# Interleaving the last feed-forward of a four-stage network with the end of its attention stack

## The chip, the cores and the metric

The kernel runs on one core of one Trainium2 chip. The metric is the device time of one execution in microseconds (us). Before the change its median over three runs is 3018.09 us (3016.32 to 3019.29). The engines are named as the profile names them: PE is TensorE (PEld its weight loads), DVE is VectorE, ACT is ScalarE, POOL is GpSimd, SP is SyncE, which here only issues DMAs.

## The reference, cut to what matters

Four stages follow each other, each added to its input: a Mamba block, a mixture of experts, a stack of six attention layers, and a gated feed-forward whose inputs and weights are quantized to FP4 in blocks of 16. The change concerns the end of the third stage and the whole fourth.

```
# six layers over (4 sequences of the batch seen as) 2 x 1024 tokens, 128 wide, 16 heads of 8
def layer(h, p):
    w_avg = softmax(q k^T / sqrt(8)).mean(heads)
    new_w = softmax(w_avg + rel)
    h1 = ln(h + new_w @ h);  h2 = ln(h1)
    ff = relu(h2 @ w1.T + b1) @ w2.T + b2
    return ln(h2 + ff)
x = x + stack(layernorm(x))
# last stage; fp4(x): per block of 16, scale = max|x| / 6, round x / scale to E2M1, times scale
xn = layernorm(x)
h  = silu(fp4(xn) @ fp4(w_gate).T) * (fp4(xn) @ fp4(w_up).T)     # 352 wide
x  = x + fp4(h) @ fp4(w_down).T
```

## The kernel before, in words

There are 2 sequences of 1024 tokens, that is 16 tiles of 128 tokens (X holds them). Every engine has its own program, written out in order; semaphores tie them together.

**The attention stack.** One loop over `STEPS` (line 172) steps runs on each engine. A step q of the first 768 (`PAIRS`) handles a pair of head groups of a block of query rows: PE computes the scores (line 650) into three PSUM tiles in turn, DVE takes the negated row maximum (1251), ACT the exponentials with their sum (922), DVE the reciprocal of the sums (1261), POOL a small diagonal matrix from it (1498), and PE the weighted sum over heads (661). All that follows per block, per tile and per half batch ("half", 4 tiles) is cut into pieces. Three tables, `BLOCK_DUE`, `TILE_DUE` and `HALF_DUE` (lines 150 to 171), say at which step after its block, tile or half is through, and at which of two places within a step, each engine issues each piece; `due()` (175) reads them. An engine executes its pieces strictly in that order. The pieces of a half, in the order of their dependencies:

- `evac` (ACT 884), `rel0 rel1` (POOL 1440), `turn` (DVE 1204), `attend0` to `attend3` (PE 594), `add1 bn0` (DVE 1209 to 1216): the second softmax and its product, per tile.
- `pv0 pw0 ln00..ln07` (POOL 1418 to 1456): statistics and application of the first layer norm; `bn10..13` (DVE 1228), `pv1 pw1 ln10..ln17` (POOL): the second; `hb0 hb1` (POOL 1460): adds the bias of the feed-forward.
- `h2t` (PE 599), `h2c` (ACT 887), `ff1_00` to `ff1_31` (PE 606, four quarters), `re0` to `re3` (ACT 895, one after each quarter; a quarter waits for the `re` before it, since all use PSUM bank 7), `ff2_0` to `ff2_7` (PE 613), `add2` (DVE 1220), `bn20..23` (DVE 1228), `pv2 pw2 ln20..ln27` (POOL): the layer's own feed-forward and third layer norm.
- in the last layer `fin` (POOL 1482) adds the result to X; it stands where `sp00` of the other layers stands, 42 steps after the half is through.

There are 24 halves (`HALF_N`); the last four (20 to 23) are the last layer's. Half 23 is the last half batch: it is through with step 767, so all its pieces come after the last pair, each waiting for the one before. SP loads the last stage's weights (1579, 1580) once the scores of half 22 are all made.

**After the loop** the engines do, in order: DVE quantizes the gate and up weights (768 columns) and the down weights (352 columns) with `fp4_dve` (1230 to 1242: nine instructions, 1234 the block maximum, 1235 to 1237 the scale, 1238 the division, 1239 to 1242 the rounding by adding and subtracting a power of two); POOL multiplies each by its scale (`requant_pool`, 1487); PE transposes them (686, 689), ACT copies them out (932 to 935). Then comes fence 3: every engine signals PE, PE signals back (522), and SP waits too. The fence is there because the last stage's buffers (XN, XQ, XQT, QA, QP, HH, HQ ...) lie in memory that the attention's tiles also use.

**The last stage** runs in whole phases. Layer norm of all 16 tiles (`ln_dve`, `ln_pool`, `ln_act`: statistics on DVE 987 to 998, the power -1/2 on POOL 1322, half the tiles applied on ACT 753); four quantizations of 4 tiles each (DVE `quant`, POOL 1487); four transposes (PE 699, ACT 941); then 8 groups of 2 tiles: `gate_up` (PE 709, ACT Silu 949, DVE product 1288), quantization of the 704 columns (DVE, then POOL 1487) and `down` (transposes PE 721, copies ACT 958 and 959, matmuls PE 728, residual add on DVE 1294). A store of 2 tiles per group (SP 1613) ends it.

```
            for grp in range(NG + 1):
                if grp + 1 < NG:
                    gate_up(grp + 1)
                if grp < NG:
                    e.wait_ge(s["swiglu"], 2 * grp + 2)
                    quant(4 + grp, ...)
                if grp:
                    down(grp - 1)
```

Of the kernel before, what the change touches and what calls it, by code (L numbers as in the profile page):

```python
# [20 lines left out]

LNQ = {"ln5": 0}
# [204 lines left out]
class Chain:  # L227
# [1474 lines left out]
```

## Time and profile before

| what | value |
|---|---|
| median of three runs | 3018.09 us |
| the profiled execution | 3021.18 us |
| its span, first to last instruction | 3019.3 us |
| mean granted clock of PE | 0.963 of full |
| busy: PE, DVE, ACT, POOL | 2612.8, 2557.9, 2365.6, 1331.9 us |
| last exponential of the attention ends | 2832.8 us into the span |
| from there to the end | 186.5 us |

The profiled execution took 3.1 us more than the median; 1.9 us of it lie outside the span. "Granted clock" is the share of its full rate at which PE ran in a stretch: 1.00 is 2.4 GHz and 0.50 is 1.2 GHz, the two levels there are, and a value between is a mix. Two engines can be busy at once, so shares of a stretch don't add up to its length.

### The profile page before, as it was taken

What the parts mean: (1) busy time and instruction counts of PE and PEld (TensorE: products, weight loads), DVE (VectorE), ACT (ScalarE), POOL (GpSimd) and SP (SyncE); (2) the same over time, 40 slices, a digit from 0 to 9 for tenths busy, and PEclk for the clock granted to TensorE, in tenths of its full rate; (3) what the DMA queues carried; (4) which work ended last, traced back from release to release, by engine and by line L of the source; (5) the groups of instructions that cost most, each with busy time, mean ns of one, the idle gap of its engine ahead of it and who ended that gap; (6) DMA issues with size and microseconds to landing.
All of it is one profiled execution on the core that took longest, in us unless ns stands there. A gap on an engine that the chain in (4) does not pass through costs nothing.

```text
span 3019.3 us, 80481 instructions
## 1 busy us (share of the span) xinstructions
PE 2612.8 (87%) x31023; PEld 1417.2 (47%) x31023; DVE 2557.9 (85%) x4100; ACT 2365.6 (78%) x4152; POOL 1331.9 (44%) x3035
## 2 busy tenths in 40 slices
PE   6888899978989889998899988898988998888636
PEld 3444576734444444444444444444444444444324
DVE  4888736489999999989998989989999998999556
ACT  5877543469889989988998989889998998999511
POOL 2111202124445664455654556645566545655421
PEclk8999999989999999999999999999999999999857
DMA  2000001322322213212223223222232232210000
GB/s 61 1 1 1 15 1 22 47 63 26 44 38 34 44 33 43 44 31 41 44 33 44 36 36 49 37 34 40 32 59 33 29 44 33 39 18 10 1 0 14
DMA packets 86783, 94.55 MB, mean 31 GB/s; under 512 B 4592, under 2 KB 84736, under 8 KB 85632
## 3 DMA queue, kind: packets, MB, share of 16 engines
q1 hardware_dynamic: 86400, 89.41, 19.0%
q8 instruction: 245, 4.01, 0.6%
q14 instruction: 138, 1.13, 0.2%
HBM read 69.47 MB, written 19.92 MB: 30 GB/s over the span
## 4 chain that ended last, share of the span: by engine, by line
PE 46%; issue 17%; DVE 15%; POOL 6%; ACT 6%; DVEq 0%; POOLq 0%; ACTq 0%
PE bank L661 12%; PE bank L650 10%; DVE NM L1251 9%; PE bank L594 5%; ACT E L922 4%; PE bank L576 3%; PE bank L566 3%; PE bank L606 3%; PE bank L613 2%; PE bank L631 1%; DVE st L1228 1%; POOL acc L1440 1%; POOL HB L1456 1%; POOL HB L1453 1%; ACT acc L884 1%
## 5 line engine op out<-in xcount | busy, mean ns | idle before, releaser
L1251 DVE TENSOR_REDUCE NM<-bank 128x1 f32<-128x1024 f32 x1536 | 1809.0, 1210 | 128.2 <-PE bank L650 123.3
L922 ACT ACTIVATE E<-bank,NM 128x1024 f32<-128x1024 f32 x1536 | 1709.8, 1116 | 223.2 <-DVE NM L1251 222.0
L661 PE MATMUL bank<-E,dg 128*32 128x256 f32 x12288 | 970.8, 385 | 96.8 <-ACT acc L884 73.7
L650 PE MATMUL bank<-KS,QS 128*32 128x512 bf16 x12288 | 961.6, 383 | 79.4 <-ACT E L922 50.6
L1498 POOL TENSOR_TENSOR dg<-mask,RZ 128x64 f32<-128x64 f32 x768 | 225.0, 293 | 833.7 <-DVE RZ L1261 713.0
L661 PEld LDWEIGHTS bank<-E,dg 128*32 128x32 f32 x12288 | 346.0, 109 | 428.6 <-issue 192.5
L650 PEld LDWEIGHTS bank<-KS,QS 128*32 128x32 bf16 x12288 | 320.2, 96 | 481.5 <-ACT E L922 296.6
L1440 POOL TENSOR_TENSOR acc<-acc,rel 128x256 f32<-128x256 f32 x384 | 273.1, 732 | 150.9 <-ACT acc L884 150.7
L922 ACT ACTIVATION_READ_ACCUMULATOR E<-bank,NM 128x1 f32 x1536 | 304.7, 198 | 0.0
L594 PE MATMUL bank<-H,ET 128*128 128x129 f32 x1536 | 225.3, 289 | 7.8 <-issue 4.8
L594 PEld LDWEIGHTS bank<-H,ET 128*128 128x128 f32 x1536 | 188.1, 192 | 89.7 <-issue 80.7
L1192 DVE SCALAR_TENSOR_TENSOR EO<-bank,OH,EO 128x128 f32<-128x128 f32 x256 | 72.0, 344 | 132.2 <-PE bank L576 132.0
L870 ACT ACTIVATE HS<-bank,cst 128x512 f32<-128x512 f32 x128 | 87.3, 686 | 112.4 <-PE bank L566 112.3
L1204 DVE STREAM_TRANSPOSE ET<-acc 128x512 f32<-128x512 f32 x192 | 133.4, 695 | 20.7 <-POOL acc L1440 20.7
L503 PE MATMUL bank<-hC,ident 128*128 128x512 f32 x256 | 142.7, 641 | 8.4 <-DVE XS L1042 7.1
L576 PEld LDWEIGHTS bank<-W,HS 128*128 128x128 f32 x1024 | 124.2, 192 | 30.4 <-issue 29.7
L825 ACT ACTIVATE dBT<-UT,BT 128x256 f32<-128x256 f32 x256 | 108.6, 495 | 25.7 <-PE bank L487 25.2
L884 ACT ACTIVATE acc<-bank 128x512 f32<-128x512 f32 x192 | 114.6, 597 | 15.0 <-PE bank L661 5.8
L576 PE MATMUL bank<-W,HS 128*128 128x128 f32 x1024 | 124.6, 275 | 0.0
L566 PE MATMUL bank<-RTr,W 128*128 128x512 f32 x256 | 121.5, 597 | 0.1
L613 PEld LDWEIGHTS bank<-WL,UB 128*128 128x128 f32 x768 | 96.9, 195 | 51.8 <-issue 49.6
L613 PE MATMUL bank<-WL,UB 128*128 128x128 f32 x768 | 119.1, 295 | 2.0 <-issue 1.1
(226 smaller groups left out, 2750.2 us busy)
## 6 DMA issues: line engine op xcount, KB each, us to landing
KS<-scratch SPq DMA_DIRECT2D x216, 128.0 KB
QS<-scratch SPq DMA_DIRECT2D x216, 128.0 KB
scratch<-UB SPq DMA_DIRECT2D x24, 768.0 KB, 3.7
WL<-in_wl SPq DMA_DIRECT2D x6, 1091.0 KB, 18.3
X<-in_x SPq DMA_DIRECT2D x4, 256.0 KB, 5.9
W<-in_moe_w SPq DMA_DIRECT2D x1, 1024.0 KB, 8.3
out<-X SPq DMA_DIRECT2D x8, 128.0 KB, 1.8
rel<-in_rel SPq DMA_DIRECT2D x1, 960.0 KB, 4.8
```

The source lines that it names most:

```text
L503: PE_.matmul(pb(c), ident[:, :], hC[:, n % 4, :], start=(n % 32 < 2), stop=(n % 32 >= 30)).then_inc(s["y"], 1)
L566: PE_.matmul(pb(2 * (n % 2) + hc), W1[:, ex, hc * 128:hc * 128 + 128], RTr[:, toks(j)], start=True, stop=True).then_inc(s["moe_up"], 1)
L576: inst = PE_.matmul(pb(4 + q % 2)[:, t * 128:t * 128 + 128], HS[:, q % 3, hc, t * 128:t * 128 + 128], W2[:, ex, hc, :], start=(hc == 0), s ...
L594: inst = PE_.matmul(o[:, 0:129], ET[:, i, :], H[:, n // 8 % 3, i, :], start=(i == 0), stop=(i == 7))
L613: inst = PE_.matmul(o[:, t * 128:t * 128 + 128], fT[:, fc, t * 128:t * 128 + 128], wl(l, "w2", fc * 128, 128), start=(fc == 0), stop=(fc = ...
L650: inst = PE_.matmul(bank[x % 3][32 * i:32 * i + 32, k * 512:k * 512 + 512], QS[:, half % 2, 4 * hq + i, r0:r0 + 32], KS[:, b, 4 * hq + i, ...
L661: inst = PE_.matmul(pb(6)[32 * k:32 * k + 32, 256 * grp:256 * grp + 256], dg[:, x // 2 % 3, x % 2, :], E[:, x % NE, :].rearrange("p (i k c ...
L884: A_.activation(acc[:, n % 2, :], pb(6), ACT.Exp, scale=1.0 / NHEAD).then_inc(s["evac"], 1)
L922: A_.activation(E[:, x % NE, :], bank[x % 3][:, :], ACT.Exp, bias=NM[:, x % 4:x % 4 + 1], accum_out=ZS[:, pair % 4, j:j + 1]).then_inc(s[" ...
L1251: V.tensor_reduce(NM[:, x % 4:x % 4 + 1], bank[x % 3][:, :], AX.X, ALU.max, negate=True).then_inc(s["rowmax"], 1)
L1440: G.tensor_tensor(y, y, rel_of(n % 16 * 64 + 32 * grp), ALU.mult).then_inc(s["rel"], 1)
L1498: G.tensor_tensor(dg[:, pair % 3, :, :], mask[:, :].unsqueeze(1).to_broadcast([128, 2, 32]), RZ[:, pair % 4, :].unsqueeze(2).to_broadcast( ...
```

## The change

The last feed-forward is cut into pieces too, and a fourth table, `LAST`, says at which step (counted from step 768; negative ones lie inside the attention) and place each engine issues them. The loop runs 70 steps past the pairs instead of 50. Fence 3 is gone. The pieces, with j a group of 4 tiles for those of two letters and digits 0 to 3 (`ls`, `pr`, `nx`, `qt`, `rq`, `tq`, `xq`) and a group of 2 tiles, 0 to 7, for the others:

- `wq00`..`wq17` (DVE): the eight instructions of each of the two weight quantizations, one piece each, at steps -14 to -7; `wr0`, `wr1` (POOL) at -10 and -6; `wt` (PE, ACT): transposes and copies of the weights, on PE at step 1, between the last two weighted sums.
- `ls` statistics (DVE), `pr` power -1/2 and bias (POOL), `nx` application of all tiles (ACT), `qt`/`rq` quantization (DVE/POOL), `tq`/`xq` transposes and copy (PE/ACT), `gu` gate and up matmuls (PE), `si` Silu (ACT), `sw` product (DVE), `qh`/`rh` quantization (DVE/POOL), `ht`/`hc` transposes and copies, `dn` down matmuls (PE), `rd` result into X (ACT).
- The subtraction that ended each quantization on DVE moves to POOL (a `tensor_tensor` before the scaling). The residual is added by PE (`ident` times X into the same PSUM bank) and no longer by DVE; ACT copies the sum into X.
- The buffers lie in KS, the keys' memory; HT has 4 slots instead of 2. Bank 6 is handed between `tq` and `dn` (`sixth_bank()`).
- `fin` of the last layer's halves stands at (39, "f") instead of (42, "d").

```
+LAST = {"PE": {(1, "g"): "wt", (10, "g"): "tq0", (13, "g"): "gu0", (16, "g"): "gu1", (18, "h"): "tq1", (19, "h"): "ht0",
+               (22, "h"): "gu2 ht1", (26, "h"): "tq2", (28, "g"): "dn0 gu3", (28, "h"): "dn1 ht2", (29, "g"): "gu4 dn2",
+               (30, "g"): "ht3 gu5 dn3 ht4", (40, "g"): "tq3 dn4 gu6 ht5 dn5 gu7", (41, "g"): "ht6 dn6 ht7 dn7"},
+        "ACT": {(3, "a"): "nx0 nx1 wt", (10, "a"): "xq0", (13, "a"): "si0", (16, "a"): "si1", (18, "b"): "xq1", (19, "b"): "hc0",
+                (22, "b"): "nx2 si2 hc1", (26, "b"): "xq2", (28, "b"): "rd0 si3 rd1 hc2", (29, "b"): "si4 rd2",
+                (30, "b"): "nx3 hc3 si5 rd3 hc4", (40, "b"): "xq3 rd4 si6 hc5 rd5 si7", (41, "b"): "hc6 rd6 hc7 rd7"},
+        "DVE": {(-14, "m"): "wq00", (-14, "e"): "wq01", (-13, "m"): "wq02", (-13, "e"): "wq03", (-12, "m"): "wq04",
...
+                (-7, "e"): "wq17", (0, "e"): "ls0 ls1", (7, "m"): "qt0", (12, "m"): "qt1", (14, "m"): "sw0 qh0",
+                (19, "m"): "sw1 qh1 ls2", (20, "m"): "qt2", (21, "m"): "sw2 qh2", (31, "m"): "sw3 qh3 ls3", (32, "m"): "sw4 qh4 qt3",
+                (33, "m"): "sw5 qh5", (34, "m"): "sw6 qh6 sw7 qh7"},
+        "POOL": {(-10, "d"): "wr0", (-6, "d"): "wr1", (3, "d"): "pr0 pr1", (10, "d"): "rq0", (17, "f"): "rq1 rh0",
+                 (20, "d"): "rh1 pr2", (22, "d"): "rq2", (29, "d"): "rh2", (39, "f"): "pr3 rh3 rh4 rq3 rh5 rh6 rh7"}}
```

In the same counting (steps from 768) half 23's own pieces stand at: `attend` 4 and 5, `h2t` 16, `ff1` 17 to 22, `ff2` 23 to 27 (PE); `h2c` 17, `re0` to `re3` at 18, 19, 20, 23 (ACT; a due piece goes before one of `LAST` at the same place); `add1 bn0` 6, `bn1x` 10 and 11, `add2` 28, `bn2x` 29 and 30 (DVE); first norm 6 to 9, second 11 to 15, `hb` 16 and 17, third 30 to 38, `fin` 38 (POOL). Half 22's `fin` is at 6.

```
                 for n, p in due("DVE", q, "m"):
                     post_dve(e, n, p)
                 rowmax(2 * q + 2)
+                for p in last("DVE", q, "m"):
+                    ffn_dve(e, own, p)
                 for n, p in due("DVE", q, "e"):
                     post_dve(e, n, p)
...
-            fence_dve(e, 3)
-            ffn_dve(e, own)
...
-        def requant_pool(e, cut, value, dst, x, sc, done):
+        def requant_pool(e, cut, value, dst, x, c, sc, own, done):
             n = sc.shape[1]
             e.wait_ge(cut, value)
+            own.then(G.tensor_tensor(x, x, c, ALU.subtract))
             G.tensor_tensor(dst.rearrange("p (n k) -> p n k", k=16), x.rearrange("p (n k) -> p n k", k=16),
                             sc.unsqueeze(2).to_broadcast([128, n, 16]), ALU.mult).then_inc(done, 1)
...
-            V.tensor_tensor(x, x, c, ALU.subtract).then_inc(done, 1)
+            else:
+                V.tensor_tensor(x, x, c, ALU.add).then_inc(done, 1)
...
+            elif p[:2] == "pr":
+                e.wait_ge(s["ln_bn"], 10 * j + 10)
+                own.then(G.tensor_tensor(lrs[:, w], lva[:, w], mhalf[:, 0:4], ALU.pow))
+                G.tensor_tensor(lnb[:, w], lnm[:, w], lrs[:, w], ALU.mult).then_inc(s["ln_nb"], 1)
...
+                    PE_.matmul(pb(6 + t)[:, 0:128], ident[:, :], X[:, i, :], start=True, stop=False)
                     for c in range(3):
                         w = min(128, I_ - c * 128)
-                        inst = PE_.matmul(pb(6 + k)[:, 0:128], HT[0:w, k, c, :], wdT[0:w, c, :], start=(c == 0), stop=(c == 2))
+                        inst = PE_.matmul(pb(6 + t)[:, 0:128], HT[0:w, i % 4, c, :], wdT[0:w, c, :], start=False, stop=(c == 2))
                     inst.then_inc(s["down"], 1)
```

## Rows read from the trace of the kernel before

**Rows 1.** The page: busy share in 40 slices of 75.5 us, tenths.

```profile
DVE  4888736489999999989998989989999998999556
...
PEclk8999999989999999999999999999999999999857
```

**Rows 2.** Stretches: from:to, length, each engine's busy us, PE clock, DMA share, GB/s.

```profile
2790.00:2815.00 25.00, 24.31 (x337) 12.87 (x340) 22.37 (x32) 23.65 (x42) 6.08 (x14) 1.00 0.01 2
...
2832.90:2860.70 27.80, 5.09 (x41) 3.77 (x33) 3.29 (x10) 0.60 (x1) 23.28 (x51) 0.65 0.00 0
2860.70:2880.00 19.30, 15.22 (x68) 9.91 (x68) 0.03 (x1) 3.35 (x5) 1.21 (x2) 0.53 0.01 1
2880.00:2893.50 13.50, 0.00 (x0) 0.00 (x0) 7.21 (x14) 0.00 (x0) 10.71 (x19) 0.58 0.00 0
2893.50:2903.60 10.10, 2.37 (x11) 1.84 (x11) 3.43 (x10) 1.36 (x5) 2.33 (x4) 0.50 0.00 0
2903.60:2935.10 31.50, 4.41 (x17) 2.89 (x17) 25.97 (x84) 5.96 (x13) 8.56 (x8) 0.50 0.00 1
2935.10:3019.30 84.20, 57.26 (x208) 39.19 (x208) 54.32 (x104) 17.00 (x49) 11.07 (x8) 0.72 0.04 13
```

The engines of a stretch stand in the order PE, PEld, DVE, ACT, POOL.

**Rows 3.** Stretches: the first eight DVE instructions of the 768 and 352 column quantization.

```profile
2881.48:2886.56 5.08, 0.00 (x0) 0.00 (x0) 4.81 (x9) 0.00 (x0) 4.42 (x10) 0.57 0.00 0
2895.04:2898.22 3.18, 0.00 (x0) 0.00 (x0) 2.90 (x8) 0.00 (x0) 0.00 (x0) 0.50 0.00 0
```

**Rows 4.** Timeline, PE: transposes of the weights (start, us).

```profile
2899.67 1.54 PE L686 MATMUL bank<-ident,QS 128*128 128x128 f32 x6 [19.74 <-POOL QS L1487]
2901.01 0.85 PE L689 MATMUL bank<-ident,QS 128*128 128x128 f32 x3
```

**Rows 5.** Timeline, POOL: norms of half 23; in brackets the idle time before.

```profile
2842.21 0.21 POOL L1418 TENSOR_TENSOR smp<-st 128x4 f32<-128x4 f32 x1 [0.99 <-DVE st L1216]
...
2844.10 1.02 POOL L1433 TENSOR_TENSOR smp<-smp,mhalf 128x4 f32<-128x4 f32 x1
2845.20 0.20 POOL L1435 TENSOR_TENSOR smp<-smp 128x4 f32<-128x4 f32 x1
...
2852.15 0.21 POOL L1418 TENSOR_TENSOR smp<-st 128x4 f32<-128x4 f32 x1 [0.60 <-DVE st L1228]
```

**Rows 6.** Timeline, POOL: the third norm's power and product, beside DVE's weight quantization.

```profile
2883.55 2.03 POOL L1433 TENSOR_TENSOR smp<-smp,mhalf 128x4 f32<-128x4 f32 x1
2885.66 0.94 POOL L1435 TENSOR_TENSOR smp<-smp 128x4 f32<-128x4 f32 x1
```

**Rows 7.** Groups by line and form, 2800 to 3020 us: busy us, mean ns, idle before.

```profile
L709 PE MATMUL bank<-QS,XQT 128*128 128x352 f32 x64 | 27.4, 591 | 0.7 <-ACT XQT L941 0.7
...
L1487 POOL TENSOR_TENSOR HQ<-QA,QC 128x704 f32<-128x704 f32 x8 | 11.1, 1384 | 66.4 <-DVE QA L1242 66.4
...
L1487 POOL TENSOR_TENSOR XQ<-QA,QC 128x512 f32<-128x512 f32 x4 | 4.2, 1058 | 17.3 <-DVE QA L1242 17.3
```

**Rows 8.** Timeline, PE: a quarter of the last half's `ff1`, all of its `ff2`.

```profile
2862.55 1.98 PE L606 MATMUL bank<-hT,WL 128*64 128x256 f32 x8 [0.78 <-ACT hT L887]
...
2873.68 6.25 PE L613 MATMUL bank<-WL,UB 128*128 128x128 f32 x32 [0.88 <-ACT UB L895]
```

**Rows 9.** Timeline: transposes of four tiles, their copy.

```profile
2933.30 1.09 PE L699 MATMUL bank<-ident,XQ 128*128 128x128 f32 x4 [3.79 <-POOL XQ L1487]
2934.42 0.60 ACT L941 ACTIVATE XQT<-bank 128x512 f32<-128x512 f32 x1 [4.28 <-PE bank L699]
```

**Rows 10.** Stretches: the first eight DVE instructions of a 512 and a 704 column quantization.

```profile
2912.76:2916.67 3.91, 0.00 (x0) 0.00 (x0) 3.64 (x8) 0.00 (x0) 0.00 (x0) 0.50 0.00 0
2943.66:2948.45 4.79, 1.60 (x6) 0.68 (x4) 4.52 (x9) 0.93 (x2) 0.00 (x0) 1.00 0.00 0
```

**Rows 11.** Timeline, PE and DVE: transposes of the last group's first tile; the last addition.

```profile
3010.64 0.90 PE L721 MATMUL bank<-ident,HQ 128*128 128x128 f32 x3
...
3016.78 0.29 DVE L1294 TENSOR_TENSOR X<-bank,X 128x128 f32<-128x128 f32 x1 [2.63 <-PE bank L728]
```

More of the change, by code:

```diff
@@ L170, with last, quant_order, sixth_bank @@
                 (31, "d"): "pv2", (33, "d"): "pw2", (35, "f"): "ln20", (36, "d"): "ln21", (36, "f"): "ln22",
[1 row of a table removed]
[1 row of a table added]
                 (42, "d"): "sp00 sp01", (42, "f"): "sp02 sp03 sp04", (43, "d"): "sp05", (43, "f"): "sp06 sp07",
                 (44, "d"): "sp08 sp09", (44, "f"): "sp10 sp11 sp12 sp13", (46, "d"): "sp14", (47, "d"): "sp15"}}
-STEPS = PAIRS + 50
+STEPS = PAIRS + 70
+LAST = {"PE": {(1, "g"): "wt", (10, "g"): "tq0", (13, "g"): "gu0", (16, "g"): "gu1", (18, "h"): "tq1", (19, "h"): "ht0",
[13 rows of a table added]
+def last(engine, step, place):
+    return LAST[engine].get((step - PAIRS, place), "").split()
+def quant_order():
+    order = [x for at in LAST["DVE"] for x in LAST["DVE"][at].split() if x[:2] in ("qt", "qh")]
+    assert order == [x.replace("rq", "qt").replace("rh", "qh") for at in LAST["POOL"] for x in LAST["POOL"][at].split() if x[:2] in ("rq", "rh")]
+    return {x: i for i, x in enumerate(order)}
+def sixth_bank():
+    table, before = {}, ("evac", BLOCKS)
+    for x in [x for at in LAST["PE"] for x in LAST["PE"][at].split()]:
+        if x[:2] in ("tq", "dn"):
+            table[x] = before
+            before = ("xqt", int(x[2]) + 1) if x[0] == "t" else ("resid", GT * int(x[2]) + 1)
+    return table
 def due(engine, step, place):
@@ L184, in due @@
                     out.append((half, p))
-                elif p == "sp00":
-                    out.append((half, "fin"))
+            elif p == "fin":
+                if half >= HALF_N - 4:
+                    out.append((half, p))
             elif half >= 0:
@@ L231, in __init__, with count, then @@
         self.e, self.sem, self.n = e, sem, 0
-    def then(self, inst):
+    def count(self, inst):
         inst.then_inc(self.sem, 1)
         self.n += 1
+    def then(self, inst):
+        self.count(inst)
         self.e.wait_ge(self.sem, self.n)
@@ L676, in attention_pe @@
                     scores(2 * q + 4)
+                for p in last("PE", q, "g"):
+                    ffn_pe(e, p)
                 for n, p in due("PE", q, "h"):
@@ L1277, in quant @@
                 if u >= 2:
                     e.wait_ge(s["requant"], u - 1)
-                fp4_dve(e, own, src, dst, n, QA[:, k, 0:n], QP[:, k, 0:n], QC[:, k, 0, 0:n // 16], QC[:, k, 1, 0:n // 16], s["cut"])
-            for j in range(4):
-                quant(j, XN[:, 4 * j:4 * j + 4, :].rearrange("p n d -> p (n d)"), XQ[:, 4 * j:4 * j + 4, :].rearrange("p n d -> p (n d)"), 512)
-            def gate_up(grp):
+                n = 4 * D if p[1] == "t" else GT * I_
+                for i in range(8):
+                    fp4_dve(e, own, i, src, n, QA[:, k, 0:n], QP[:, k, 0:n], QC[:, k, 0, 0:n // 16], QC[:, k, 1, 0:n // 16], s["cut"])
+            else:
@@ L1522, in gpsimd @@
         def gpsimd(e):
+            own = Chain(e, s["pool"])
             scan_pool(e)
```

314 lines of the change are left out of this document (150 added, 164 removed), and 4 rows, old and new, of tables (HALF_DUE, LAST).

## The prediction

> **What bounds the kernel now.** I read first the page's slices [rows 1]: DVE is at nine tenths nearly everywhere, and only the last three slices fall to five and six, with PE's clock at 0.8, 0.5 and 0.7. So the time on offer lies behind the last exponential, at 2832.8 us; 186.5 us follow it. Then the stretches [rows 2], which cut these by what ends last: **A** 27.8 us, POOL 23.28 busy (softmax end and two norms of half 23); **B** 19.3 us, PE 15.22 (its feed-forward); **C** 13.5 us, POOL 10.71 (third norm, `fin`); **D** 10.1 us (weights scaled, transposed, fence); **E** 31.5 us, DVE 25.97 (norm and quantization of 16 tiles); **F** 84.2 us, PE 57.26 and DVE 54.32 (eight groups). In A to D every engine but one waits, while 12 of the 16 tiles could already go through E and F: the halves 20 and 21 are through long before, half 22's `fin` needs only POOL.
>
> **Is there room?** DVE needs 3.29 + 25.97 + 54.32 us for A, E and F, about 1.6 for `add2` and its statistics, and gives away 12 subtractions (up to 0.9) and 16 additions of 0.29 [rows 11]: some 71 us. POOL needs 23.28 + 10.71 + 1.21 + 8.56 + 11.07 = 55, plus the subtractions, bounded below by the scaling of the same size, 4 x 1.06 + 8 x 1.38 = 15 [rows 2, 7]: 70. PE is at 84 us, mostly at the half clock. No engine fills the 123 us that I arrive at, so chains decide, and I follow them stage by stage, each in the order in which its engine issues.
>
> **Weights inside the attention.** Sixteen pieces, 5.08 + 3.18 = 8.3 us of DVE [rows 3], go into steps -14 to -7. There PE is busy 24.31 of 25 us and DVE 22.37 [rows 2]: DVE has 2.6 us to give. I charge 8.3 - 2.6 = **+5.6**; bounds +2 (the row maxima run a little ahead of ACT, and spacing closes up) and +10 (`wr0`, two POOL instructions over 768 columns, each longer than the 1.38 us of 704 [rows 7], stands ahead of the diagonals and of `rel` in step -10). POOL's 6.08 busy us of 25 cover it otherwise. The two loads are issued at 2740.8, 50 us ahead. `fin` three steps earlier costs nothing for halves 20 and 21.
>
> **A.** (1) `wt` stands on PE between the last two weighted sums, and `evac` waits for the second. Its transposes took 1.54 + 0.85 us at clock 0.50 [rows 2, 4]; here PE comes from clock 1.00, so half: +1.2 (bounds 1.2 and 2.4). ACT's copies lie beside POOL's work. (2) POOL gets `pr0 pr1` ahead of the rest of half 22's norm: twice a power (1.02) and a small product (0.2 to 0.4 with its wait) [rows 5]: +2.8. (3) Half 22's `fin` only changes place, from within the first norm to ahead of it; but the 0.99 us that POOL idled there are used up: -1.0. (4) `rq0` stands ahead of the second norm: 2 x 1.06 [rows 7], less the 0.60 us of idling there [rows 5]: +1.5. (5) DVE's `qt0`, `qt1` and `qh0` now run beside POOL's norms. Rows show what that does: the power took 1.02 us alone and 2.03 beside the weight quantization, the product 0.20 and 0.94 [rows 5, 6]. Two such hits of 1.0 and one of 0.5: +2.5 (bounds 0 and the 7.3 below). `ls0 ls1` (3.3 us) fit before `turn`. A: **+7.0**.
>
> **B.** PE's queue, and ACT's behind it. Between the quarters stand now: `tq1` then `xq1` ahead of `re1`; `ht0` then `hc0` ahead of `re2`; `gu2 ht1` then `hc1` ahead of `re3`; `tq2` inside `ff2`. At the full clock: 1.09 / 2 and 0.60 [rows 9]; two tiles' transposes, 0.90 / 2 each [rows 11], and a copy of 0.65, estimated from the 0.60 of rows 9; eight matmuls (27.4 / 64 = 0.43 us apiece at F's clock 0.72, so 0.3 [rows 2, 7]), again 0.9 and 0.65; 0.55 for `tq2`. Sum 1.15 + 1.55 + 3.95 + 0.55 = 7.2 us; with PE's share doubled, at the half clock, 11.6 to 12.5, of which I take 11.6. Against this PE is kept busier: if it reaches 2.4 GHz, `h2t`, four quarters of 1.98 and 6.25 of `ff2` [rows 8], 15.3 us together, halve. All fast: 19.3 + 7.2 - 7.6 = 18.9; all slow: 30.9. Stretch B had the clock at 0.53 although PE was busy 15.22 of 19.3 us [rows 2], so I take 26, nearer to slow: **+6.7**.
>
> **C.** `rh2`, 2 x 1.38 [rows 7], stands ahead of `pv2` and waits for `qh2`, which follows `si2` late in B; the statistics hide some 0.7 of it: +2.1. The collision with DVE is there already (the weights now, `qh3` then): +0.5. **+2.6**.
>
> **D.** Gone: **-10.1**. Nothing takes its place; `gu0` waits for `tq0` behind `rq0`, well after `wt`'s copies.
>
> **E.** Behind `fin` only one group of four tiles is left: `ls3` 1.7 (E's 25.97 less four quantizations of 4.6 leaves 1.9 a group, of which the new group does less); then, in DVE's order, `sw4` 1.0 (F's 54.32 less eight times 5.5, less the additions, is 0.4 to 0.5 a tile) and `qh4` 4.79 before `qt3` 3.91 [rows 10]; `rq3` 2.1; `xq3` behind `tq3` and what PE has ahead of it (`ht3 gu5 dn3 ht4`), 2.2. With 2.3 for `qt3`'s wait on `rh3` (POOL 2 x 1.38, itself behind `pr3`): 18.0 for 31.5. **-13.5**.
>
> **F.** Six of eight groups are through or under way. Left, at the full clock: `gu6` 2.4, `dn4` 2.5 (57.26 - 27.4 is 1.9 a tile at 0.72, 1.3 at 1.00; less the transposes' 0.45, plus a third for `ident`, 1.2), the last Silu and product 0.9; `qh6` 4.79; `sw7 qh7` 5.8 (DVE does not wait for POOL here); `rh7` 2.8; transposes, copies and down matmuls of the last two tiles, 6.14 from rows 11 at mixed clocks, plus one matmul of `ident` per tile, some 5.5 at a better clock; copy, store and end 2.5 as today (3016.78 to 3019.3); 0.8 for collisions: 28.0 for 84.2. **-56.2**.
>
> Sum: 5.6 + 7.0 + 6.7 + 2.6 - 10.1 - 13.5 - 56.2 = **-57.9 us**. The profiled execution would go from 3021.18 to 2963.3; it stands 3.1 us over the median, so the median goes to 3018.09 - 57.9 = **2960.2**. I round up to 2961 for waits between pieces that no row prices.
>
> **A rule against the change.** What rows 5 and 6 show is a POOL instruction held up by DVE's. The Trainium skill, page "SBUF — State Buffer", section "Who interferes with whom", says that DVE and GpSimd share a port pair, taken for a whole instruction by a DVE instruction with two SBUF inputs or in a two-port mode, so that the other blocks fully. The block maximum would stay free, and four of the eight instructions would block. Worked out from rows that is the next rival.
>
> **Rivals.**
> - *Full exclusion of POOL by DVE.* If every one of the four wide instructions (about 2.2 us per 512, 2.9 per 704 columns, roughly 0.6 of rows 10) adds its whole length to POOL's chain: A 7.3 instead of 2.5, C 2.9 for 0.5, E and F 5 for about 2: +10, **2971**. For: rows 6. Against: POOL's small instructions between fit beside the block maximum, and a blocked instruction delays only if it is on the chain.
> - *PE stays at 1.2 GHz behind the attention.* Its queue then ends E and F too: B +4.9, `dn` and `gu` of 4.7 us a pair instead of 2.4, six pairs in a row on the chain: about +27 with the waits that follow, **2988**. For: clock 0.50 in D and E, 0.53 in B. Against: 0.72 in F, where PE is busier [rows 2], and 1.00 in the second of rows 10.
> - *Everything fits.* No collisions (-5), weights at +2 (-3.6), B all fast (-7): **2945**.
> - *Slower: the weights' pieces break the attention's round.* Each of 16 sits between two row maxima, and ACT and PE wait for those. To end slower, each must cost 57.9 / 16 = 3.6 us more than charged, over a step of some 2.9 us. For: PE and DVE are both nearly full there, and each piece waits for the one before. Against: that one was issued half a step earlier and is done. At 4 us each the time is 3018 - 58 + 64 = **3024**.
>
> **Chances.** Forecast 0.46, exclusion 0.17, slow PE 0.17, all fits 0.18, broken round 0.02, in half of which it would stop within the measurement's 0.2%. Range: the forecast's own is 2950 to 2972; to leave out no more than 2 in 10 it must reach to both neighbours: 2943 to 2989. A measurement of this kernel tells apart some 0.2% (6 us): faster 0.98, same 0.01, slower 0.01.
>
> **What would show it.** The last L922 activation ends at 2838.4 (+5.6), later than 2843 if the round breaks. `h2t` starts 12.6 us later than its 2860.7; `add2` at about 2899; `fin` of half 23 ends near 2915; from there to the end of the span some 46 us. POOL's power beside `qt1` is longer than 1.02. The clock from 2895 on tells forecast from slow PE. I am wrong in kind if PE or DVE is idle for more than 8 us between `fin` of half 23 and the last `qh7`, or if a queue waits in B for a piece of `LAST` that is itself late.

## The result, and the profile after

The changed kernel takes **2965.45 us** (median of four runs, 2960.66 to 2967.91), the kernel before, beside it on the same chip, 3018.16 us (3016.32 to 3019.29): a ratio of 0.9824, 95% interval 0.9807 to 0.9841. 52.7 us are gone; 2961 was forecast, with 2943 to 2989 as the range. The profiled execution took 2967.9 us (span 2966.1, clock 0.975).

The page's slices of the changed kernel (74.2 us each now), which answer to [rows 1]:

```profile
DVE  4888836389989998999999999999999899999976
...
PEclk8889999989999999999999999999999999999988
```

DVE's last three slices read 9, 7, 6 for 5, 5, 6, and no slice of PE's clock is under 8. The stretches below are cut at the same marks as A, B, C in [rows 2]: last exponential, `h2t`, `add2`, end of half 23's `fin`; the last two cut what is left at the end of `xq3`. Columns as there.

```profile
2843.10:2878.08 34.98, 13.91 (x71) 8.66 (x62) 18.53 (x53) 8.70 (x20) 30.40 (x57) 0.66 0.00 1
2878.08:2905.94 27.86, 16.66 (x104) 11.89 (x104) 22.56 (x42) 8.65 (x22) 14.25 (x12) 0.94 0.00 1
2905.94:2920.25 14.31, 10.09 (x62) 8.23 (x62) 8.19 (x16) 4.22 (x13) 12.87 (x21) 1.00 0.09 27
2920.25:2938.75 18.50, 8.99 (x40) 6.64 (x40) 17.70 (x35) 5.71 (x17) 9.60 (x9) 0.72 0.02 7
2938.75:2966.10 27.35, 19.10 (x98) 15.65 (x98) 13.94 (x24) 7.11 (x25) 9.16 (x6) 0.81 0.07 20
```

A, B and C each grew, D is gone, and E and F, 115.7 us in [rows 2], are 18.5 + 27.4. In DVE's column 3.29 + 0.03 + 7.21 us have become 18.5 + 22.6 + 8.2: that is the overlap, in numbers. The attention is read from a mark in code that the change left alone, SP's load of the gate and up weights, to the end of the last exponential; before, and after:

```profile
2740.78:2832.85 92.07, 83.43 (x1200) 42.76 (x1204) 86.81 (x128) 83.94 (x146) 46.26 (x111) 1.00 0.03 8
```

```profile
2744.47:2843.10 98.63, 85.09 (x1200) 41.89 (x1204) 94.58 (x144) 84.15 (x146) 51.05 (x115) 1.00 0.03 8
```

| term | forecast | profile |
|---|---|---|
| weights inside the attention | +5.6 | +6.6 (92.07 to 98.63) |
| A | +7.0 | +7.2 (27.8 to 35.0) |
| B | +6.7 | +8.6 (19.3 to 27.9) |
| C | +2.6 | +0.7 (13.6 to 14.3) |
| D, E, F | -79.8 | -79.9 (125.7 from `fin`'s end to 45.9) |
| sum | -57.9 | -56.8 |

The span itself fell by 53.2 only: the mark came 3.7 us later in this profile (2740.78, then 2744.47), and all code before it does the same work in both kernels. In the twelve runs below it lies between 2736.9 and 2749.4, and the changed kernel itself, run again, had it at 2741.2. So **the place of the attention's end varies by some us from run to run, whatever the change**, and the experiments are read behind the last exponential, where the same code gives more nearly the same length: 186.4 us before, 123.0 after. (The repeat below is within 0.3 us up to `fin`'s end, and 2.7 us longer at the end.)

### The profile page after: what moved, and what is told of

Same layout as the page of the kernel before. It is cut to its first block, busy times and chain, and to the rows that moved or that the text cites. A ratio compares the mean times of both kernels' runs of the same rounds, so it can differ in the third digit from the quotient of the medians.

```text
span 2966.1 us, 80538 instructions
## 1 busy us (share of the span) xinstructions
PE 2606.5 (88%) x31053; PEld 1412.8 (48%) x31053; DVE 2551.9 (86%) x4061; ACT 2372.2 (80%) x4175; POOL 1355.7 (46%) x3052
## 4 chain that ended last, share of the span: by engine, by line
PE 45%; issue 18%; DVE 15%; POOL 7%; ACT 5%; DVEq 0%; POOLq 0%; ACTq 0%
PE bank L706 12%; PE bank L695 10%; DVE NM L1274 9%; PE bank L639 5%; PE bank L621 4%; ACT E L959 4%; PE bank L611 3%; PE bank L651 3%; PE bank L658 2%; PE bank L676 1%; POOL acc L1457 1%; DVE st L1239 1%; POOL HB L1473 1%; ACT acc L921 1%; POOL HB L1470 1%
## 5 line engine op out<-in xcount | busy, mean ns | idle before, releaser
L706 PE MATMUL bank<-E,dg 128*32 128x256 f32 x12288 | 969.4, 385 | 95.9 <-ACT acc L921 75.5
L621 PEld LDWEIGHTS bank<-W,HS 128*128 128x128 f32 x1024 | 124.2, 192 | 30.4 <-issue 29.7
L621 PE MATMUL bank<-W,HS 128*128 128x128 f32 x1024 | 124.6, 275 | 0.0
L658 PE MATMUL bank<-WL,UB 128*128 128x128 f32 x768 | 118.0, 293 | 4.3 <-ACT UB L932 4.3
L658 PEld LDWEIGHTS bank<-WL,UB 128*128 128x128 f32 x768 | 95.8, 193 | 53.3 <-issue 47.8
```

The costliest lines, as they stand in the source:

```text
L621: inst = PE_.matmul(pb(4 + q % 2)[:, t * 128:t * 128 + 128], HS[:, q % 3, hc, t * 128:t * 128 + 128], W2[:, ex, hc, :], start=(hc == 0), s ...
L658: inst = PE_.matmul(o[:, t * 128:t * 128 + 128], fT[:, fc, t * 128:t * 128 + 128], wl(l, "w2", fc * 128, 128), start=(fc == 0), stop=(fc = ...
L706: inst = PE_.matmul(pb(6)[32 * k:32 * k + 32, 256 * grp:256 * grp + 256], dg[:, x // 2 % 3, x % 2, :], E[:, x % NE, :].rearrange("p (i k c ...
```

## The experiments

Theory: the gain is the overlap of the last stage with half 23's chains, which costs the attention and A to C some 23 us of queueing and pays with all of D and most of E and F. Twelve kernels ran, one of them the changed kernel once more, four at a time beside the kernel before, each four on another chip. So times are compared within a four, and otherwise by their ratio to the kernel before.

### Nothing beside the attention's end

The same pieces without the fence, but every step of `LAST` from 0 on put behind half 23's own pieces:

```
+for _e in LAST:
+    LAST[_e] = {(k[0] + (50 if k[0] >= 0 else 0), k[1]): v for k, v in LAST[_e].items()}
-STEPS = PAIRS + 70
+STEPS = PAIRS + 120
```

> The changed kernel with every piece of LAST that stood at step 0 or later moved 50 steps back, in the same order, so that the whole last feed-forward comes behind fin of half 23; no fence, the buffers and the weights' place as changed. Theory 1 (the gain is the overlap with half 23's end): stages A to C go back to their 60.6 us, and behind fin stand some 105 us (115.7 of E and F less what DVE gave away), so the time is near 3003 us, some 15 under the old kernel. Theory 2 (fence, weights and the moved subtraction and addition made most of the gain): the time stays within 15 us of the changed kernel's 2965.

3000.95 us (2995.98 to 3003.37), ratio 0.9929 (0.9912 to 0.9946). Its stretches, cut at the last exponential, `fin`'s end and the end:

```profile
2845.44:2902.14 56.70, 19.60 (x118) 12.91 (x109) 7.64 (x35) 3.96 (x7) 32.87 (x72) 0.61 0.00 1
2902.14:3001.60 99.46, 55.93 (x256) 42.52 (x256) 68.32 (x132) 30.88 (x89) 38.45 (x33) 0.76 0.04 11
```

156.2 us behind the last exponential, where the changed kernel has 123.0. So 33 of the gain are the overlap alone (A to C fall back to 56.7 us, but 99.5 follow; about 60.6 and 105 were expected). The other 30 of the 63 that the tail lost come from what this kernel keeps: no fence, the weights quantized earlier, and pieces of several groups in turn instead of whole phases; these were not taken apart. A part of A to C's fall below the 60.7 us of the kernel before can be named: C took 11.2 us here and 13.6 there, since DVE's weight quantization no longer runs beside the third norm, and POOL's power and product take 1.02 and 0.20 us for the 2.03 and 0.94 of [rows 6].

### The weights behind the attention

`wq`, `wr` and `wt` moved out of the attention, between half 23's pieces (and the down weights' work buffers moved off those of the last norm, which are in use by then):

```
-... (-14, "m"): "wq00", ... (-7, "e"): "wq17", (0, "e"): "ls0 ls1", (7, "m"): "qt0", ...
+... (0, "e"): "ls0 ls1", (5, "m"): "wq00 ... wq07", (7, "m"): "qt0", (8, "m"): "wq10 ... wq17", ...
-"POOL": {(-10, "d"): "wr0", (-6, "d"): "wr1", (3, "d"): "pr0 pr1", (10, "d"): "rq0", ...
+"POOL": {(3, "d"): "pr0 pr1", (10, "d"): "rq0 wr0 wr1", ...
```

> The changed kernel with the weights quantized behind the last pair: DVE's pieces behind turn and behind qt0, POOL's wr0 and wr1 behind rq0, the transposes behind tq0. Theory 1 (the sixteen pieces cost the attention 6.5 us, as DVE is full there): the last exponential comes 6 us earlier, POOL's two pieces add 5 us to the norms' chain, the time is 1 to 2 us lower, not to be told from the changed kernel. Theory 2 (they were hidden in the attention): 5 us slower than the changed kernel, some 2970.

2968.23 us (2965.78 to 2969.63), ratio 0.9822 (0.9807 to 0.9837). Stretches, cut at the mark, the last exponential and the end:

```profile
2743.62:2835.80 92.18, 83.53 (x1204) 42.73 (x1204) 86.84 (x129) 84.02 (x146) 46.23 (x111) 1.00 0.03 8
2835.80:2967.80 132.00, 72.11 (x373) 53.69 (x365) 91.12 (x183) 34.74 (x95) 81.76 (x107) 0.75 0.03 9
```

The attention is back at 92.2 us, as before the change, so the weights cost it **6.4 us**, and the tail costs 9.0 more. By these two profiles their place inside the attention is worth 2.6 us, no more than the changed kernel's own tail differs between two profiles (123.0 and 125.7, below); at the end of `fin` there is nothing left of it, 6.6 us later here (83.8 for 77.2). It is worth so little because DVE's work on them is paid in either place: it is busy 7.8 us more in the attention of the changed kernel (94.6 for 86.8), and here 10.2 us more in the tail (91.1 for 80.9).

### The clock in B, in the kernel before

The kernel before, with ten matmuls without use (352 columns, result unread) ahead of the last `h2t`:

```
+                if n == HALF_N - 1:
+                    e.wait_ge(s["exp"], N)
+                    e.wait_ge(s["tln"], 12 * n + 4)
+                    for i in range(10):
+                        PE_.matmul(pb(i % 4)[:, 0:352], ident[:, :], E[:, i % 4, 0:352], start=True, stop=True)
```

> The kernel before, with ten idle matmuls of 352 columns (their results are read by nobody) put on PE ahead of h2t of half 23, beside POOL's second norm. Theory 1 (the changed kernel's stage B ran at the full clock because gu0 and gu1 stand ahead of h2t): the quarters of ff1 take 1.08 instead of 1.98 us and ff2 3.3 instead of 6.3, stage B falls from 19.3 to about 12, the time to about 3011. Theory 2 (the clock follows only what comes later): nothing moves, or h2t is late by up to 3 us: 3018 to 3021.

3017.53 us (ten runs, 3004.19 to 3026.86), ratio 0.9983 (0.9966 to 0.9999). Its PE timeline (start, us), beside [rows 8]:

```profile
2855.00 8.51 PE L601 MATMUL bank<-E,ident 128*128 128x352 f32 x20 [10.49 <-POOL ZA L1461]
2863.91 0.66 PE L604 MATMUL bank<-ident,HB 128*128 128x128 f32 x4 [0.40 <-POOL HB L1461]
2865.34 1.08 PE L611 MATMUL bank<-hT,WL 128*64 128x256 f32 x8 [0.78 <-ACT hT L892]
...
2872.91 5.44 PE L618 MATMUL bank<-WL,UB 128*128 128x128 f32 x32 [0.88 <-ACT UB L900]
```

A quarter of `ff1` takes 1.08 us for 1.98: with PE busy ahead of it, B runs at clock 0.88 and lasts 14.5 us for 19.3. `ff2` took 5.44 us and not the expected 3.3: the clock was 1.00 over the quarters, in which PE was busy 5.0 of 9.0 us, and 0.69 in `ff2`. The tail is 5.9 us shorter than before (180.5 us), the median 4.1 us under the 3021.66 of the kernel before beside it; some 7 were expected. That is the state in which the changed kernel finds itself: `gu0` and `gu1` (from 2870.25) stand directly ahead of its `h2t`, and its B has clock 0.94. **So the forecast's B was right by luck.** It took 26 us, between all fast (18.9) and all slow (30.9). PE was fast; the other 9 us are something else.

### What B waits for

The changed kernel's B: `h2t` on PE, then its ACT, from the profile's timeline.

```profile
2888.99 1.08 PE L651 MATMUL bank<-hT,WL 128*64 128x256 f32 x8 [1.31 <-ACT UB L932]
2890.01 2.63 PE L756 MATMUL bank<-QS,KS 128*128 128x352 f32 x8
2893.04 0.87 PE L766 MATMUL bank<-ident,KS 128*128 128x128 f32 x6 [0.40 <-POOL KS L1505]
2898.19 3.83 PE L658 MATMUL bank<-WL,UB 128*128 128x128 f32 x20 [4.28 <-ACT UB L932]
```

```profile
2894.28 1.65 ACT L982 ACTIVATE KS<-X,KS 128x128 f32<-128x128 f32 x4 [5.34 <-POOL KS L1541]
...
2897.36 0.69 ACT L932 ACTIVATE UB<-bank,WL 128x512 f32<-128x512 f32 x1
```

The fourth quarter of `ff1` ends at 2890.07, but its `re3` (L932) runs at 2897.36: ahead of it in ACT's queue stands `nx2` (L982), which waits 5.34 us for POOL's `pr2`, itself behind `rh1`. `ff2` (L658) therefore starts at 2898.19, and PE, idle for 4.28 us before it, is slower in it too: clock 0.63 over its first 20 matmuls, 3.83 us. Two kernels change the order. The first puts `nx2 si2 hc1` behind `re3`, and `ht1` behind `ff2`; the second also sends `ls2` and `pr2` ahead:

```
-PE  (22, "h"): "gu2 ht1", (26, "h"): "tq2"     +PE  (22, "h"): "gu2", (27, "h"): "ht1 tq2"
-ACT (22, "b"): "nx2 si2 hc1"                   +ACT (23, "b"): "nx2 si2 hc1"
second kernel, besides:
-DVE (19, "m"): "sw1 qh1 ls2"                   +DVE (19, "m"): "ls2 sw1 qh1"
-POOL (20, "d"): "rh1 pr2"                      +POOL (20, "d"): "pr2 rh1"
```

> The changed kernel with `nx2 si2 hc1` on ACT one step later, behind `re3`, and `ht1` on PE behind `ff2` (at `tq2`). Theory (stretch B took 27.9 us because queues wait for late pieces of the last stage: ACT for POOL's `pr2` ahead of `nx2`, with `re3` behind it, and PE for `rh1` ahead of `ht1`): the last piece of `ff2` ends about 5 us earlier, at 55 us behind the last exponential instead of 60, and ACT's `re3` directly follows the fourth quarter. `add2` gains less if DVE's queue (`qh1`, `qt2`, `qh2` ahead of it) then ends last. Rival (B was long because PE had more matmuls, at whatever clock): `ff2` ends at 59 to 60 us, since nothing is taken away. Time 2961 by the theory if add2 follows, 2965 if DVE's queue holds it or by the rival.

> The kernel with `re3` first, and besides `ls2` ahead of `sw1 qh1` on DVE and `pr2` ahead of `rh1` on POOL, so that `nx2` is ready sooner. Theory: `si2` comes sooner, so that `qh2`, the last DVE piece ahead of `add2`, ends about 5 us earlier than the 62.9 us behind the last exponential that it took; `add2` starts at 57 to 58 us for 62.8. Rival (DVE's queue is full by then: `qh1`, `qt2` and `qh2` are bound by DVE's own work and by its collisions with POOL, not by the Silu): `add2` stays at 61 us or later. Time 2960 by the theory, 2965 by the rival.

First: 2962.15 us (2957.74 to 2971.68), ratio 0.9817 (0.9794 to 0.984). `ff2` ends 53.1 us behind the last exponential where it ended at 61.3, eight earlier and more than expected (all its 32 matmuls took 3.73 us, with no pause before them), and yet `add2` starts at 62.8 as ever. Its DVE timeline says why:

```profile
2901.39 0.89 DVE L1263 TENSOR_TENSOR KS<-KS 128x704 f32<-128x704 f32 x1
2902.20 0.68 DVE L1231 TENSOR_TENSOR HB<-bank,ZA 128x512 f32<-128x512 f32 x1
```

`add2` (L1231) follows `qh2` (L1263) without a gap: a second queue ends at the same moment as the first. Second: `add2` at 60.1 and `fin`'s end at 74.5 for 77.2, so DVE's queue did wait for the Silu, by 2.7 us and not 5. Its time is 2967.07 us (2962.12 to 2972.97), ratio 0.983 (0.9809 to 0.9852): nothing of it reaches the end. The span's end comes 123.1 us behind the last exponential, as in the changed kernel.

### Stretch A

```
-PE  (1, "g"): "wt"         +PE  (1, "h"): "wt"
-POOL (3, "d"): "pr0 pr1"   +POOL (2, "d"): "pr0", (3, "d"): "pr1"
```

> The changed kernel with `wt` on PE one place later (behind the last weighted sum instead of between the last two) and `pr0` one step earlier on POOL (before the four `rel` pieces instead of behind them), `pr1` where it was. Theory (what stretch A gained is plain queueing: each instruction that stands ahead of the chain costs its own length): the last weighted sum starts 1.2 us earlier after the last exponential, and `pr0`'s 1.2 us leave the chain, so `h2t` starts 32.5 us after the last exponential instead of 34.9. Rival (A's extra 7 us are mostly collisions between DVE and POOL, which stay): `h2t` still starts 34.5 to 35 us after it. Time by the theory 2963, by the rival 2965.5; three rounds hardly separate these, the marks of the profile do.

2957.42 us (2951.52 to 2965.55), ratio 0.9791 (0.9768 to 0.9814). `h2t` starts at 33.75 for 34.98: 1.2 us and not 2.4. The two edits had the same idle time in view. In the changed kernel POOL waits 1.32 us for `evac`, which waits for the weighted sum behind `wt`; with `evac` 1.3 us earlier, `pr0` fills just that time. The span's end is at 124.6, again not earlier; the profiled run is the slowest of its four.

### The order behind `fin`

```
-DVE "sw3 qh3 ls3", "sw4 qh4 qt3"    +DVE "sw3 qh3 sw4 qh4", "ls3 qt3"
-POOL "pr3 rh3 rh4 ..."              +POOL "rh3 pr3 rh4 ..."
-ACT "nx3 hc3 ...", "xq3 rd4 si6"    +ACT "hc3 nx3 ...", "xq3 si6 rd4"
-PE  "tq3 dn4 gu6 ..."               +PE  "tq3 gu6 dn4 ..."
```

> The changed kernel with another order behind `fin`: DVE `sw3 qh3 sw4 qh4` and then `ls3 qt3`, POOL `rh3` before `pr3`, ACT `hc3` before `nx3`, PE `gu6` before `dn4`. Theory (from `fin` on a chain of the last group decides: `ls3 pr3 nx3 qt3 rq3 tq3 xq3 gu6`, in which `sw4 qh4`, 7.5 us, stand ahead of `qt3`, and `dn4`, 3.4 us, stands ahead of `gu6`): `gu6` starts 3 us earlier behind `xq3`, and `qh4` fills DVE while it waits for POOL's `fin`, so the stretch from `fin`'s end to the end of the span falls from 45.9 to about 41. Rival (the stretch is bound by DVE's amount of work, the same in any order): it stays between 44.5 and 46. Time 2960.5 by the theory, 2965 by the rival.

2963.15 us (2956.27 to 2967.04), ratio 0.9814 (0.9795 to 0.9833); from `fin`'s end to the end 47.1 us for 45.9. The theory's 5 us are not there. Two lines each of its DVE and its PE show where they went:

```profile
2918.14 2.29 DVE L1257 TENSOR_TENSOR KS<-KS 128x704 f32<-128x704 f32 x1
2920.47 1.59 DVE L1259 TENSOR_SCALAR KS<-KS 128x704 uint32<-128x704 uint32 x1
```

```profile
2935.03 1.11 PE L746 MATMUL bank<-ident,KS 128*128 128x128 f32 x4 [4.62 <-POOL KS L1505]
2936.83 4.95 PE L756 MATMUL bank<-QS,KS 128*128 128x352 f32 x8 [0.69 <-ACT KS L985]
```

The division took 2.29 us for its usual 0.89 and the next one 1.59 for 0.53, beside POOL's `rh3`. And `gu6` (L756) starts 96.4 us behind the last exponential for 99.2, but takes 4.95 us where it took 2.53: PE had been idle for 4.62 us, and it is at the half clock.

### The clock at the end

In three variants the front had won up to 2.7 us, in the fourth the order behind `fin` had changed, and in all four the end stayed at 123 to 125. The next kernel leaves all orders as they are and fills PE's idle time behind `fin`:

```
+            if p == "tq3":
+                e.wait_ge(s[SIXTH[p][0]], SIXTH[p][1])
+            for _ in range({"ht3": 24, "tq3": 12, "ht6": 16, "ht7": 4}.get(p, 0)):
+                PE_.matmul(pb(6 if p == "tq3" else 4)[:, 0:128], ident[:, :], ident[:, :], start=True, stop=True)
```

> The changed kernel with idle PE time behind `fin` filled by matmuls without use (`ident` times `ident`, 128 columns, into a bank that is free): 24 ahead of `ht3`, 12 ahead of `tq3`, 16 ahead of `ht6`, 4 ahead of `ht7`. The last four variants all ended 123 to 125 us behind the last exponential although `h2t`, `add2` or `fin` came up to 2.7 us earlier; theory: what the front wins is given back by PE's clock in the last 30 us (in one of them `gu6` took 3.81 us where it took 2.53, in another the last transposes 1.54 where they took 0.88). Then this run keeps the clock over 0.9 from `tq3` to the end: `ht3`'s group goes at 0.82 and 2.5 us where it took 1.54 and 4.55, `dn4` ends 1.3 us earlier, and from `fin`'s end to the span's end there are 43 to 44.5 us for 45.9. Rival (the end is bound by DVE's and POOL's own work, the clock is only beside it): it stays between 45.5 and 46.5. Time 2963 to 2964 by the theory, 2965 to 2966 by the rival.

> The changed kernel itself, once more, beside the others on this chip. If the profile's marks are steady, `h2t` starts 34.9, `add2` 62.8 and the span's end 123.0 us behind the last exponential, each within 0.5 us; the last exponential's own place varies by some us from run to run, with the part of the kernel that the change leaves alone. Time 2965, ratio to the kernel before 0.982.

Filled: 2961.09 us (2952.89 to 2969.3), ratio 0.9815 (0.9792 to 0.9838). The changed kernel again: 2964.08 us (2957.16 to 2967.34), ratio 0.9822 (0.9803 to 0.9841). The last stretches of the two, cut 18.5 us behind `fin`'s end:

```profile
2940.90:2967.50 26.60, 19.78 (x138) 16.62 (x138) 13.71 (x24) 7.11 (x25) 9.17 (x6) 1.00 0.07 20
```

```profile
2935.77:2965.50 29.73, 21.41 (x98) 17.45 (x98) 13.94 (x24) 7.67 (x25) 9.16 (x6) 0.73 0.06 18
```

Up to `fin`'s end the repeated kernel matches its first profile within 0.3 us (`h2t` 34.99, `add2` 63.13, `fin` 77.43), but its end comes at 125.7, not at 123.0: the last stretch took 29.7 us at clock 0.73, where the first profile had 27.4 at 0.81. So the same kernel differs with itself by 2.4 us in 30. DVE is busy 13.94 us in both and POOL 9.16; what differs is the clock, and PE's and ACT's busy time. With PE filled, the stretch has clock 1.00 and takes 26.6; from `fin`'s end to the end there are 45.1 us, between the theory's 43 to 44.5 and the rival's 45.5. The mark that all would repeat within 0.5 us was wrong, for the end alone, and this bears on the variants above. Three of them (stretch A, the second kernel of B, the order behind `fin`) have clock 0.73 to 0.79 in this stretch, like the repeated kernel, and their tails of 123.1 to 124.8 us lie between the 123.0 and 125.7 of the changed kernel itself. So one profile can't show at the end a gain of 1 to 3 us at the front: the spread that goes with the clock covers it. Both kernels with PE filled, this one and the last below, have clock 1.00 in this stretch; neither was repeated, so that their own spread is not known. By itself filling wins little, 0.8 us against the better of the two profiles: DVE's and POOL's chain ends not much earlier than PE's.

### All of it together

The orders of stretches A and B, with the subtraction of each quantization back on DVE; first that subtraction alone:

```
-            own.then(G.tensor_tensor(x, x, c, ALU.subtract))
+            elif i == 7:
+                inst = V.tensor_tensor(x, x, c, ALU.add)
+            else:
+                V.tensor_tensor(x, x, c, ALU.subtract).then_inc(done, 1)
```

> The changed kernel with the subtraction that ends each quantization back on DVE. Theory 1 (neither DVE nor POOL alone sets the tail, the chain passes from one to the other): DVE's chains get 0.7 to 0.9 us longer per quantization, POOL's 1.3 to 1.7 shorter, the sum is within 3 us of the changed kernel. Theory 2 (POOL sets it): 6 us or more faster. Theory 3 (DVE sets it): 6 us or more slower.

2963.13 us (2957.06 to 2965.79), ratio 0.9803 (0.9785 to 0.9821); the end at 119.7 for 123.0 and, repeated, 125.7; `fin` ends at 75.0, 2.2 us earlier, where the repeat differed by 0.3. DVE is 3.3 us busier behind the last exponential (84.2 for 80.9), POOL 17.6 less (58.7 for 76.3). The ratio is not told apart from the changed kernel's 0.9824, which is what the first of the three theories says.

> The changed kernel with the orders that each gave something at the front taken together (`wt` behind the last weighted sum, `pr0` one step earlier, `nx2 si2 hc1` behind `re3`, `ht1` behind `ff2`, `ls2` ahead of `sw1 qh1`, `pr2` ahead of `rh1`) and the subtraction of each quantization back on DVE. Theory (terms add as long as they lie on one chain): `h2t` at 33.7 us behind the last exponential, `add2` 1.2 + 2.7 us earlier than 62.8, so 59, less another 1 for POOL's lighter `requant`; `fin` ends at 72 to 73, and the span's end comes 118 us behind the last exponential. Rival (the clock gives it back, or DVE is full now): the end stays at 120 to 123. Time 2960 by the theory, 2963 by the rival.

> The kernel of all these orders together with the matmuls without use of the run with a filled PE. Theory (front and clock together): the gain of the orders is kept to the end, which comes 115.5 to 117 us behind the last exponential; time 2957 to 2958, 2 to 4 us under the kernel without the matmuls. Rival (DVE and POOL bind the end): the same as without them.

Without filling: 2955.71 us (five runs, 2948.32 to 2960.68), ratio 0.9793 (0.9773 to 0.9813). With: 2956.99 us (2954.54 to 2959.47), ratio 0.9802 (0.9786 to 0.9818). Both have `h2t` at 32.8, `add2` at 58.2 and `fin`'s end at 69.4 us behind the last exponential, 7.8 earlier than the changed kernel. The end comes at 119.4 and at 115.4. PE's timeline of the last two tiles, without filling and with it:

```profile
2951.43 0.98 PE L766 MATMUL bank<-ident,KS 128*128 128x128 f32 x6 [2.11 <-POOL KS L1508]
2952.61 0.79 PE L778 MATMUL bank<-X,ident 128*128 128x128 f32 x2 [0.21 <-ACT KS L1003]
2953.19 1.49 PE L781 MATMUL bank<-QS,KS 128*128 128x128 f32 x6
```

```profile
2951.87 0.87 PE L770 MATMUL bank<-ident,KS 128*128 128x128 f32 x6 [0.89 <-POOL KS L1512]
2953.05 0.49 PE L782 MATMUL bank<-X,ident 128*128 128x128 f32 x2 [0.31 <-ACT KS L1007]
2953.37 0.83 PE L785 MATMUL bank<-QS,KS 128*128 128x128 f32 x6
```

A tile's down matmuls take 0.83 us for 1.49. The profiled tail is 4.0 us shorter with filling, but the two medians, 1.3 us apart the other way, don't tell the kernels apart: the runs of each spread over 12 and 5 us. Both medians lie below that of the changed kernel run beside them (2964.08), by 8.4 and 7.1 us, and the tails by 3.6 and 7.6 us against its better profile; the intervals of the ratios overlap its own (0.9803 to 0.9841), so that a gain of some 7 us is likely and not certain.

## Why the prediction was right, point by point

- **What bounds it** (chains behind the last exponential, not an engine's amount): held. The kernel with all pieces behind has the same work and takes 156 us for 123. The amounts were put too low, though: DVE was busy 80.9 us for the "some 71", by collisions (last section), and POOL 76.3 for 70, also since its subtractions took 1.67 and 1.26 us for the 1.38 and 1.06 that bounded them.
- **The sum**, -57.9: the profile's -56.8 is the better of two. The repeated kernel's tail of 125.7 us gives some -54, and so do the medians: -52.7, and 53.7 us below the kernel before in the repeat (3017.81 and 2964.08). So the forecast was some 4 to 5 us too good, well inside its range; which terms were off stands below.
- **Weights in the attention**, +5.6: 6.4 to 6.6. 8.3 us of DVE less the 2.6 that it had to give, worked out from two rows, was near. The missing us is probably a wait that was not priced: DVE's scale of the down weights (L1251, 22 numbers a row) took 1.40 us at 2814.34, where it takes 0.18, beside POOL's `wr0` (2814.21 to 2815.71). In the kernel with the subtraction on DVE it took 0.19, and the attention needed the same 98.6 us although two subtractions (0.96 and about 0.5) were added; no run has the one without the other.
- **A**, +7.0: 7.2, by its parts too. `wt` took 0.87 + 0.49 us, its 1.2; `pr0 pr1` 2.5 for 2.8; half 22's `fin` 1.72 us beside DVE where it took 1.17. The 2.5 for collisions came true in sum: POOL's instructions of A lasted 2.6 us longer than the shortest of their kind, but `fin` and the small ones of the norm's statistics, and not the power that was forecast.
- **B**, +6.7: 8.6, and here a step failed: "Stretch B had the clock at 0.53 although PE was busy 15.22 of 19.3 us [rows 2], so I take 26, nearer to slow". The row was of a B that nothing preceded on PE; the change puts `gu0 gu1` ahead. The clock was 0.94, and queues took the time: ACT behind `pr2`, then DVE's `qh2`. The prediction's own condition, a queue that waits in B for a late piece of `LAST`, came true, though it cost little: with ACT's wait gone, DVE's queue ends at the same moment.
- **C**, +2.6: 0.7. `rh2` ahead of `pv2` was priced at 2.1, and POOL's norm starts 1.7 us later behind `add2` (3.3 for 1.7). The term that failed is "+0.5" for the collision: it should have been negative, since the 13.6 us of before held the old one (11.2 without it, above). The 2.03 and 0.94 us of [rows 6] are 1.02 and 0.20 now, and what DVE's `qh3` holds up instead (L1470 1.23, the second L1467 1.77, for 0.72 and 0.88) is less.
- **D, E, F**, -79.8: -79.9, and -77.5 in the repeat. E 18.5 us for 18.0, F 27.4 for 28.0 and 29.7 in the repeat, so that the exact hit is luck. F's working leaves 0.36 us a tile for DVE's product and not "0.4 to 0.5"; measured it is 0.48, as the 1.0 for `sw4` has it. Inside E errors cancel: DVE's `ls3 sw4 qh4` took 9.0 us and `qt3` 5.8, 14.8 for the forecast's 11.4, by collisions; but the 2.3 for `qt3`'s wait on `rh3` never came, and `xq3` ended 1.3 us behind `rq3` for 2.2.
- **The rivals.** Full exclusion (2971) was nearer to the mechanism than its chance of 0.17 allowed, but it struck DVE more than POOL, and DVE's small instructions, which it left out, more than the four wide ones (last section); the measured time lies about midway between the forecast and this rival. Slow PE (2988) is out: clock 0.94, 1.00, 0.72, 0.81 from B on. That everything fits (2945) fails by A, B and the attention. The attention's round did not break: its last exponential ended 6.6 us later by the mark, 0.4 us a piece. (At 2843.1 it stands at the prediction's sign for a broken round, 2843; 3.7 us of that lie ahead of the mark.)
- **The marks.** `h2t` +13.7 by the same mark (12.6), `add2` 62.8 us behind the last exponential (47.1 + 7.0 + 6.7 = 60.8), end of `fin` 77.2 (60.7 + 16.3 = 77.0), 45.9 from there to the end (46; 48.2 in the repeat). The sign of the collision, POOL's power beside `qt1` longer than 1.02, could not show: `qt1` had ended (2870.84) when the power started (2871.42). Of the signs of being wrong in kind, the one on idle time came true for PE if it means the sum: 13.9 us idle between `fin`'s end and the end of `qh7`, 6.1 in the longest pause; DVE was idle 5.1. PE's three long pauses there all end with a result of POOL.

## What to carry to other kernels

When the last part of a kernel is a chain of short waits on one half batch, independent work of the next stage fills it at a low price: the tail fell from 186 to 123 us, 16.5 us of queueing included, and 6.6 us were paid in the attention. The next gain does not come from one queue: bringing `ff2` eight us forward moved `add2` by nothing, since a second queue ended at the same moment. Singly, the orders of A, those of B and the lighter POOL gave 1.2, 2.6 and 2.2 us at `fin`; together they gave 7.8. At the end of the kernel such gains are easily lost to PE's clock: in the changed kernel `gu5`, behind a pause of 9.5 us and six transposes, took 4.55 us for 2.53, and a tile's down matmuls, behind one of 3.8, 1.49 for 0.83. Compare the granted clock of a stretch before a reordering is judged, and repeat the profile.

## What was not expected of the hardware

Collisions between DVE and POOL went both ways, and mostly the one that was not forecast. The forecast counted POOL instructions held up by DVE [rows 5, 6]. Taking each instruction's time behind the last exponential over the shortest of its line and shape, POOL's were 5.1 us longer in sum in the changed kernel, DVE's 12.7; in the kernel before it was 3.1 and 1.6. Of DVE's 12.7 us, 7.5 lie in the two small scale instructions of each quantization (L1251, L1255), the rest nearly all in the four wide ones. POOL held up, beside `qt0` and `qt1`:

```profile
2855.14 1.72 POOL L1499 TENSOR_TENSOR X<-X,H 128x512 f32<-128x512 f32 x1
...
2857.79 0.65 POOL L1439 TENSOR_TENSOR smp<-smp 128x4 f32<-128x4 f32 x1
...
2870.26 0.65 POOL L1441 TENSOR_SCALAR smp<-smp 128x4 f32<-128x4 f32 x1
```

The first takes 1.17 us elsewhere, the other two 0.20. DVE held up, and POOL beside it, behind `fin`:

```profile
2922.74 0.89 DVE L1249 TENSOR_REDUCE KS<-KS 128x44 f32<-128x704 f32 x1
2923.66 1.23 DVE L1251 TENSOR_SCALAR KS<-KS 128x44 f32<-128x44 f32 x1
2924.92 0.43 DVE L1253 RECIPROCAL KS<-KS 128x44 f32<-128x44 f32 x1
2925.39 0.96 DVE L1255 TENSOR_SCALAR KS<-KS 128x44 f32<-128x44 f32 x1
```

```profile
2923.18 1.67 POOL L1504 TENSOR_TENSOR KS<-KS 128x704 f32<-128x704 f32 x1
2924.93 1.38 POOL L1505 TENSOR_TENSOR KS<-KS 128x704 f32<-128x704 f32 x1
```

DVE's 44-element scale takes 0.18 us alone; here it starts at 2923.66 and ends at 2924.89, 0.04 us after POOL's subtraction (2924.85), and the next one ends at 2926.35, after POOL's product (2926.31). The block maximum (0.89) and the reciprocal (0.43) are untouched. A wait of DVE's small instruction for a whole POOL instruction is what the Trainium skill, page "SBUF — State Buffer", section "Who interferes with whom", states: whoever issues first holds the shared pair for the whole instruction, and the other blocks. The trace agrees for these two forms. It makes the price depend on the length of POOL's instructions, and so fits the subtraction: taken from POOL, where one of 704 columns lasts 1.67 us, all twelve cost DVE 3.3 us more busy time and not their own 9.9 (8 x 0.89 + 4 x 0.69), since its other instructions are held up 6.6 us less; the tail is 3.3 us shorter than the better of the changed kernel's two. That the collisions are the reason of this gain, and not POOL's shorter queue, was not separated.
